# The row maxima of a softmax turned by one transposing transfer and sent in two, in place of a block transposition and eight transfers

## What is computed

```
q, k, v = layernorm(x), ctx, ctx            # split in 16 heads of 16
scores  = einsum('bthd,bshd->bhts', q*s, k*s)   # s = 1/sqrt(sqrt(16))
w       = softmax(scores, axis=-1)          # over the 512 keys
x       = x + einsum('bhts,bshd->bthd', w, v) @ w_proj.T + b_proj
z       = layernorm(x)
gates   = softmax over the two largest of z @ Wg.T
x       = x + sum_e gates_e * ((silu(z@W1_e.T) * (z@W2_e.T)) @ W3_e.T)
```

## The kernel before

| slot | what SyncE does (before) |
|---|---|
| 3 | rows of group 0 |
| 4 | `x_in` of two batches on (512 KB), after waiting for GpSimd's `q16` of the batch before it (`s_ql`, L570; GpSimd's instruction is L773); `v_ext` (1 MB, L591); `x2` out (512 KB) |
| 5, 6 | `x_res` (512 KB), `kt_in` (512 KB) |
| 7 | rows of group 1; then `keep_weights` c=1 |
| 9 | `k_part` and `q_part` of the next batch: 12 transfers of 128 KB |
| 11 | rows of group 2 |
| 13 | `keep_weights` c=2 |
| 15 | rows of group 3 |
| 0 | `keep_weights` c=0 of the next expert |

## Time and profile before

### The profile page before, as it was taken

The page is one execution under the profiler, slowest core; times in us unless marked ns, Lnnn a source line. Parts: engine busy times, 40 slices in busy tenths (PEclk is TensorE's granted clock), DMA queues, the critical chain, the costliest instruction groups (busy, mean ns, idle before and its releaser), DMA issues. The chain is left out here.

```text
span 912.9 us, 20228 instructions
## 1 busy us (share of the span) xinstructions
PE 804.6 (88%) x6712; PEld 499.3 (55%) x6712; DVE 604.5 (66%) x1258; ACT 550.7 (60%) x903; POOL 462.4 (51%) x424
## 2 busy tenths in 40 slices
PE   0478988989899898988989899997999999999995
PEld 0112222223223222322348799996999999999894
DVE  4888988979899897999525475553444444444552
ACT  3268878878788887758763444443444444444442
POOL 4656437797878879676715563222222222222222
PEclk9999999999999999989999999999999999999998
DMA  9484856749494774934454688988775577272722
GB/s 175 133 228 150 210 152 212 162 138 245 148 254 135 249 184 146 204 138 159 131 227 168 197 252 270 287 236 257 241 241 144 145 239 244 46 241 47 243 47 24
DMA packets 72050, 167.77 MB, mean 184 GB/s; under 512 B 11440, under 2 KB 49328, under 8 KB 67376
## 3 DMA queue, kind: packets, MB, share of 16 engines
q1 hardware_dynamic: 58544, 149.03, 53.8%
q0 software_dynamic: 13440, 17.90, 9.9%
HBM read 129.45 MB, written 42.55 MB: 188 GB/s over the span
## 5 line engine op out<-in xcount | busy, mean ns | idle before, releaser
L952 DVE TENSOR_REDUCE neg_max<-ps 128x2 f16<-128x1024 f32 x256 | 306.7, 1221 | 34.3 <-PE ps L1251 30.7
L818 ACT ACTIVATE probs<-ps 128x1024 f32<-128x1024 f32 x256 | 257.9, 1027 | 79.5 <-PE ps L1264 76.8
L745 POOL DMA_INDIRECT out<-y,aim x72 | 112.2, 1559 | 269.9 <-DVE y L1182 205.6
L1365 PE MATMUL ps<-zt,w 128*128 128x256 f16 x792 | 216.5, 273 | 6.3 <-DMA w<-w_parts 3.0
L1369 PE MATMUL ps<-zt,w 128*128 128x256 f16 x792 | 216.6, 274 | 0.0
L1367 PE MATMUL ps<-zt,w 128*128 128x256 f16 x792 | 216.6, 273 | 0.0
L853 ACT ACTIVATE silu<-ps 128x256 f32<-128x256 f32 x216 | 82.6, 382 | 200.7 <-PE ps L1369 199.5
L1164 DVE SCALAR_TENSOR_TENSOR hid<-ps,silu 128x256 f32<-128x256 f32 x216 | 91.6, 425 | 140.1 <-ACT silu L853 136.9
L1251 PE MATMUL ps<-k_stack,q_stack 48*128 48x512 f16 x512 | 104.8, 408 | 49.6 <-ACT probs L818 30.9
L1279 PE MATMUL ps<-probs,v_ext 128*32 128x512 f32 x1024 | 139.7, 618 | 4.6 <-ACT heads L887 3.5
L1264 PE MATMUL ps<-q_stack,k_stack 49*128 49x512 f16 x512 | 101.9, 397 | 16.1 <-DVE neg_max L952 9.4
(11 more groups left out here) (129 smaller groups left out, 993.7 us busy)
## 6 DMA issues: line engine op xcount, KB each, us to landing
w<-w_parts SPq DMA_DIRECT2D x36, 1408.0 KB
w<-w_parts SPq DMA_DIRECT2D x36, 768.0 KB
w_in<-in_w SPq DMA_DIRECT2D x16, 704.0 KB
z_in<-slots SPq DMA_DIRECT2D x37, 258.0 KB, 7.7
v_ext<-in_v SPq DMA_DIRECT2D x8, 1024.0 KB, 6.4
k_stack<-k SPq DMA_DIRECT2D x48, 128.0 KB, 6.8
q_stack<-qt SPq DMA_DIRECT2D x48, 128.0 KB, 7.3
w_in<-in_w SPq DMA_DIRECT2D x8, 768.0 KB
```

Source lines behind the costliest of these rows:

```text
L745: nc.gpsimd.indirect_dma_start(out=out, out_offset=bass.IndirectOffsetOnAxis(ap=aim[frm][:, t, 0:1].bitcast(U32), axis=0), in_=y[frm][:, t ...
L818: nc.scalar.activation(probs[g % 2][:, j:j + 2, k, :], pair_banks[PLACE["exp", u] % 3], ACT.Exp, scale=0.25).then_inc(s_exp, 1)
L952: nc.vector.tensor_reduce(neg_max[b % 2][:, g, c:c + 9:8], pair_banks[PLACE["max", u] % 3], AX.X, ALU.max, negate=True).then_inc(s_red, 1)
L1365: nc.tensor.matmul(dst, w[:, kk, 1, cols], z16[:, kk, 0, :], start=(kk == 0), stop=False)
```

## The change

The turning moves from VectorE to a transfer: `neg_max` and `max_t` get 128 columns per group, SyncE waits for VectorE's maxima themselves (`s_red`), and issues one transposing transfer of 128 x 128 elements of 16 bit (32 KB) in slot 3 + 4g. One slot later (4 + 4g) it waits for that transfer's end (`s_mt`) and sends the 16 wanted rows in two transfers. Within a slot the order on SyncE is: `x_in`, `k_part`/`q_part`, `v_ext`, then these transfers, then `keep_weights` and the rest.

```
-        neg_max = [sa(f"neg_max{i}", [P, 4, 32], F16) for i in range(2)]
-        max_t = [sa(f"max_t{i}", [P, 32], F16) for i in range(2)]
+        neg_max = [sa(f"neg_max{i}", [P, 4, P], F16) for i in range(2)]
+        max_t = [sa(f"max_t{i}", [P, 1, P], F16) for i in range(2)]
...
                 for g in range(4):
                     for b in due(slot, AT_MAX_ROW + 4 * g):
-                        sp.wait_ge(s_mt, b * 4 + g + 1)
-                        for k in range(4):
-                            for par in range(2):
-                                row = 64 * par + STACK
-                                to = q_stack[b % 2][row:row + 1, 2 * g:2 * g + 2, :]
-                                to = to.rearrange("p a (i k n) -> p k (a i) n", i=NT, k=4)
-                                sp.dma_start(to[:, k], max_t[g % 2][32 * k + 8 * par:32 * k + 8 * par + 8, :]
-                                             ).then_inc(s_mrow[g], 16)
+                        sp.wait_ge(s_red, b * UNITS + 8 * (g + 1))
+                        if b * 4 + g >= 2:
+                            sp.wait_ge(s_mrow[(g + 2) % 4], (b if g < 2 else b + 1) * 32)
+                        sp.dma_start_transpose(max_t[g % 2][:, :, :], neg_max[b % 2][:, g, :]).then_inc(s_mt, 16)
+                    for b in due(slot, AT_MAX_ROW + 4 * g + 1):
+                        sp.wait_ge(s_mt, (b * 4 + g + 1) * 16)
+                        for par in range(2):
+                            row = 64 * par + STACK
+                            sp.dma_start(q_stack[b % 2][row:row + 1, 2 * g:2 * g + 2, :].rearrange(
+                                "p a (i n) -> p (a i) n", i=NT), max_t[g % 2][8 * par:8 * par + 8, 0, :]
+                                ).then_inc(s_mrow[g], 16)
...
+                        if b >= 2 and s % 4 == 0 and half == 0:
+                            dve.wait_ge(s_mt, ((b - 2) * 4 + g + 1) * 16)
                         nc.vector.tensor_reduce(neg_max[b % 2][:, g, c:c + 9:8], pair_banks[PLACE["max", u] % 3],
                                                 AX.X, ALU.max, negate=True).then_inc(s_red, 1)
-                    if s % 4 == 3 and half == 1:
-                        q = b * 4 + g
-                        if q >= 2:
-                            dve.wait_ge(s_mrow[(g + 2) % 4], (b if g < 2 else b + 1) * 128)
-                        dve.wait_ge(s_red, u + 1)
-                        nc.vector.transpose(max_t[g % 2][:, :], neg_max[b % 2][:, g, :]).then_inc(s_mt, 1)
...
-                        pe.wait_ge(s_mrow[s // 4], (b + 1) * 128)
+                        pe.wait_ge(s_mrow[s // 4], (b + 1) * 32)
```

## The result

The change is slower: 946.42 us median (944.79 to 948.54, 4 runs) against 921.78 us, ratio 1.027 with a 95% interval of 1.0232 to 1.0308. That is 24.6 us by the medians. The two profiled executions stand further apart, 946.97 us (span 945.2) against 914.7 us, 32.3 us, because the profiled run of before was faster than all runs behind the median (918.77 to 924.19); sums over the traces have to meet the 32.3.

What follows compares the result with a forecast made beforehand. In the attention stage no engine alone was taken as the bound; they share the slots. 914.7 + 20.1 (group 0) + 1.0 (group 2, batch 1) - 4.1 (VectorE) = 931.7 us; +17.0 on the median gave 939, range 918 to 956.

Steps and rivals of the forecast that it cites:

- Group 0 behind `q16`, `x_in` and `v_ext`: SyncE's queue, attention stage: group 0's rows usable 7.7 us after q16 ends; batches 0 and 2 to 5 lose 20.1 us.
- It adds up over the batches: Attention stage: group 0's delays accumulate and aren't worked off, since q16 hangs on a VectorE step ending the batch before.
- Group 2 of batch 1: Rows behind the k_part and q_part transfers in the queue: near 2 us late, 1 us taken as k_part goes earlier.
- Groups 1 to 3 at nothing: Rows of the later groups: 0 beyond batch 1's 1 us, having slots to spare or time given by group 0's delay.
- The transposing transfer: SyncE's new transfer per group: 2.4 us taken from the 352 KB transfer's row, hidden at group 0.
- VectorE's gain: 32 transpositions removed from VectorE in the attention stage: 4.1 us gained, of a 10.9 us ceiling.
- The sign that VectorE's busy time falls by 6.8 us: A sign that the forecast is right: VectorE's busy time drops by 6.8 us.
- slip past large ones: Rival, DMA queue: small rows don't stand behind v_ext, usable 1.3 us after issue; median about 919 us, chance 0.15.
- The faster case: Rival: issue and packet count are what costs, so fewer SyncE issues and VectorE's gain give 914 us; chance 0.13.
- The third one: Rival: the transposing transfer takes 6.4 us and holds SyncE, 22 us above the forecast, 961 us; chance 0.08.
- the signs: Marks of a right forecast: among them, attention stage ends some 15 us later, experts' stage as long as it was.

Runs made afterwards that it cites:

- The old mechanism in the new place: Kernel before, VectorE's transposition and eight transfers kept, with all groups' rows sent one slot later, behind x_in, v_ext and keep_weights: ratio 1.039 to the kernel before.
- group 0 alone: Kernel before with only group 0's eight rows one slot later, behind x_in and v_ext: ratio 1.034 to the kernel before.
- the wait filled: The change with 16 spare matmuls ahead of TensorE's wait for group 0's rows in batches 0 and 2 to 5: 942.85 us, ratio 1.030 to the kernel before.
- weights behind: keep_weights c=0 sent behind group 0's rows: in the kernel before 1.005; in the change with rows ahead of x_in and v_ext, c=1 also later, 1.033.
- put group 0 right: The change with the two row transfers sent ahead of x_in and v_ext in slot 4 + 4g: ratio 1.017 to the kernel before.
- move 1 to 3 alone: Kernel before with only the rows of groups 1, 2 and 3 one slot later, group 0 in place: ratio 1.025 to the kernel before.
- both steps in one slot: The change with SyncE waiting at once for the transposing transfer and sending the rows right behind it, in slot 3 + 4g: ratio 1.034 to the kernel before.

## Why the prediction was right, and where its sizes were off

It said 939 us (918 to 956), slower, for the place of group 0's rows; measured are 946.42. The direction and the main mechanism are right. The size is less good than it looks: the sum starts from the trace of before and adds 17.0 us, and the traces stand 32.3 us apart. By its steps:

- **Group 0 behind `q16`, `x_in` and `v_ext`: right, in size too.** The exponential follows the end of `q16` by 7.3, 8.7, 8.0 and 8.2 us in batches 2 to 5, where 7.7 was taken. The delay that each batch adds up to its group 0 is 4.5 us in batch 0 and 2.3, 4.9, 4.7 and 4.8 in batches 2 to 5, 21.2 us in all against 20.1 forecast. The old mechanism in the new place (1.039), and group 0 alone (1.034), show that the place alone makes such a loss.
- **It adds up over the batches: right.** But for 1.2 us at group 2 of batch 1 and some tenths, nothing is given back. The ends of `q16` in batches 2 to 5 are 5.8, 9.6, 16.0 and 22.3 us later than before, about what the batch ahead had lost at its last group (6.1, 9.6, 16.4 and 22.8 us), as the forecast had it.
- **What was missing: the slots behind a stall.** Between group 0's and group 1's first exponentials the batches 2 to 6 lose another 1.5, 2.4, 1.7, 1.4 and 1.0 us, 8.0 us, where the sum had 0. In batches 2 to 5 the granted clock is at half there, for 3.4 or 6.8 us behind the stall, and in batch 4 TensorE has no idle time in it from 276 us on; in batch 6, where the clock is full, the matmuls wait 1.35 us for group 1's rows. With the wait filled the five losses are 5.2 us. The traces thus show half rate as a part of these 8 us; how large a part stays open, and the medians show no gain.
- **Batch 0 lost another 2.8 us** between groups 1 and 2, where no matmul waited for rows. It is TensorE's half rate, which lasts until 75 us in the change and until 61 in the kernel before, under a clock column that reads 1.00. Seven other kernels, too, have no wait for rows and no second half-clock stretch between these groups: the four at full rate by 64 to 67 us lose at most 0.2 us there, the three at full rate by 69, 70 and 72 us lose 1.5, 2.8 and 2.8. What decides when the full rate comes is open; it came at 70 us also with group 0 early (weights behind).
- **Group 2 of batch 1: 1.0 us forecast, 1.2 us gained.** `k_part` went out at 107.20 against 102.81, with the batch 7.3 us late by then, so 2.9 us earlier in its batch.
- **Groups 1 to 3 at nothing: right here, wrong as a reason.** I said that they have reserve. Much of it is what group 0's stall lends: put group 0 right, and 1.7% is still lost, with most of the wait at groups 1 and 2; move 1 to 3 alone, and it is 2.5%.
- **The transposing transfer: its length right, its side effects not.** From its issue to SyncE's going on, with nothing ahead, it is 2.3 us (group 3 of batch 0), against 2.4 taken from the 352 KB transfer. The Trainium skill says that such transfers are as fast as plain ones ("Advanced Engine Details and Errata", X-Bar Transpose (TRN2)). The 2.3 us don't speak against it, but no run has a plain transfer of 32 KB beside it, and the issue on SyncE is nearly twice as long as a plain one's (1.19 against 0.67 us). And the sum priced it at 0 outside its own path, while an idle one per group costs 2.9%.

```profile
79.19 1.12 SPq L597 DMA_TRANSPOSE max_t<-neg_max  x1
81.49 1.33 SPq L602 DMA_DIRECT2D q_stack<-max_t  x2
```

- **VectorE's gain, 4.1 us: not seen.** Alone it is worth 1.8 us (none to 4.7). The sign that VectorE's busy time falls by 6.8 us failed too: it fell by 2.8 us, from 604.5 to 601.7, though the 6.8 us of transpositions are gone.
- **The rivals.** Small transfers don't slip past large ones: the rows are usable when `v_ext` has landed, 0.2 us behind it in batch 4. The faster case, by coalescing, didn't come, though SyncE's issue time for the rows did fall by half. The third one, a slow transposition that holds SyncE, isn't group 0's loss, since SyncE stands at `q16` there and sends the rows at once behind `v_ext`; but SyncE does stand 75.2 us for transpositions in the change, at the other groups, and that wait is what makes both steps in one slot slow.

Together: 21.2 + 8.0 + 2.8 - 1.2 and small losses and gains in the rest, -1.7, make the stage's 29.1 us, where the signs said some 15; the experts' stage added 3.2, where they said that it stays as long as it was. From the forecast's 17.0 to the 32.3 it is 1.1 at group 0, 8.0 behind the stalls, 2.8 in batch 0, -2.2 at group 2 of batch 1, 2.4 for VectorE's gain and the rest together, and 3.2 in the experts' stage. By the medians the gap is 7.6 us, 24.6 against 17.0. That it is half as wide there comes from the profiled run of before, 7.9 us under its median, and not from the sum: it is luck. Which of the 15.3 us belong to that fast run no trace tells.

## What to carry to other kernels

Read a transfer's place in its queue before its cost: list what is issued ahead of it, with its bytes and with the waits of the issuing engine, and compare that with the time at which the reader needs it. Fewer transfers in a chain of two can be worse than many in one if each link has to pass a full line: here the issuing engine stood 75 to 152 us between the links. Where all engines are nearly full, price each group's reserve with the others' stalls removed: a group that seems to have time may be living on the stall in front of it. And check a clock column against the length of the matmuls before calling the clock full.

## What was not expected

An issue of a transposing transfer holds SyncE for 1.13 to 1.19 us at the median and up to 2.2 us, nearly twice a plain one's 0.63 to 0.67, and 32 of them with nothing waiting cost 2.9%. Around TensorE's stalls of 3 to 5 us in the change the granted clock was at half for 3.4 or 6.8 us at a time; with both steps in one slot it was 17.1 us in batch 4. And TensorE worked at half rate up to 61 us in the kernel before and up to 75 in the change, where the clock column shows nothing of it.
